# Parts of both halves stacked a batch ahead, expert rows loaded earlier, and a first layer whose sum is made by tokens

## The chip, the cores and the metric

The kernel runs on one NeuronCore of a Trainium2 chip, as one program. The metric is the device time in microseconds from start to end of one execution. A core has TensorE (matmuls and transposes into PSUM), VectorE, ScalarE, GpSimd and SyncE, which here only issues DMAs. The engines meet only at semaphores, and each runs its own instructions strictly in order.

## The reference, cut to what matters

```python
def layer0(x):                        # x: 8 x 512 x 128, layer-normed copy n; 16 heads of 8
    q, k, v = ...                     # q from n, k and v from a latent of 32; rope on q and k
    att = softmax(sum over d of q*k)  # for every token: 16 heads against 16 heads
    out = (att @ v) @ Wout + bout
    h = silu(n @ wg) * (n @ wu)       # hidden 384
    return x + out + h @ wd
def layer1(x1):
    u, z = split(norm(x1) @ in_proj)  # 256 channels each; u through a causal conv of 4 taps and silu
    dt = softplus(...)                # max(x,0) + ln(1 + exp(-|x|)), with a correction of rounding
    for t in tokens:                  # 256 channels x 16 states, a recurrence over 512 tokens
        h = exp(dt*A) * h + (dt*u) * B
        y = sum over states of h * C
    y = (y + u*D) * silu(z) @ out_proj
    return x1 + y + shared expert + the two best of 8 experts (sigmoid gates, sorted into tiles)
```

## The kernel before, in words

**Two layers, one after the other.** `layer0` walks the 8 batches of 512 tokens in a pipeline: iteration b makes the scores of batch b, the values, the gated hidden layer and the sum of batch b-1, and the next layer's norm, transposes and gate logits of batch b-2. All five engines have their lists of steps written out by hand. The sum of batch b-1 is made by channels (`project_out`: the attention and the three hidden blocks against `wout` and `wd`, 512 tokens wide, into the PSUM tile `p_acc`). ScalarE copies it and adds `bout` (`copy_sum`), TensorE transposes it back to tokens (`turn_back`, which stands behind `turn_x` and `latent` of batch b+2), and VectorE adds the residual (`add_up`, L704). VectorE also runs the routing of each group of four batches: `choose(0)` at the end of iteration 6, `place(0)` in iteration 7, `choose(1)` and `place(1)` at the end. GpSimd scatters the rows of group 0 to their experts' tiles in DRAM (`send(0, 0)` at the end of iteration 7, `send(0, 1)` at the end of iteration 8), 16 indirect DMAs each; `second_root` of the next iteration stands behind them in its queue.

**Layer 1** has a prologue for batch 1 and then, for every batch, 32 steps k. Step k works on one group of 128 (channel, state) rows by 512 tokens. TensorE spreads dt*u over the 16 states (`spread_du`, L1834, into one of two `p_du` buffers, one step ahead, free once `scan` k-1 is done). VectorE multiplies by B (`inject`, L1716) and runs the recurrence (`scan`, L1723). GpSimd multiplies by C (`times_c`, L1459), TensorE gathers. ScalarE exponentiates the decays two steps ahead (`decay`), from tiles of 1 MB that SyncE loads, 8 in a batch (`load_decays`), into 4 buffers.

dt*u is a float32 number that TensorE takes as three bfloat16 parts. `first_part` and `second_part` (ScalarE), `second_rest` (L1705) and `third_part` (L1710, VectorE) make them for one half of the channels at a time into `part`, and SyncE's `stack` moves them by 12 small DMAs into `block_in`. Half 0 of batch b+1 is made in steps 19 to 22 of batch b; half 1 in steps 5 to 8 of batch b+1 itself, since `part` and `block_in` have room for one of each.

The softplus of batch b+1 runs in steps 13 to 17: ScalarE's exponential, VectorE's 1 + e (`softplus_one`, L1691), ScalarE's logarithm, VectorE's `softplus_cut` and `softplus_end`.

**Expert tiles** run among the steps: each batch has two units of the shared expert and eight tiles of 256 routed rows, a unit every 3.2 steps. Each unit has a slot s, and its stages are placed around it: rows and weights are loaded at step s-11 (`load_tile`, SyncE: L1300 129 KB of rows, L1305 384 KB of weights), the rows are transposed at s-7 (L1850), gate at s-6, up at s-5, `half` (VectorE) at s-4, `hidden` (GpSimd) at s-3, `down` at s (L1883 for the shared expert), `weigh` (ScalarE) at s+1, and the result is stored at s+2. The last tile has slot 6 of batch 7. From step 9 of batch 7 GpSimd fetches the second group's results with 32 indirect DMAs (`fetch`, L1495); the first waits until all tiles are stored.

A wait at the head of an engine's list holds all that is behind it. TensorE's next `spread_du` stands behind the transposes and matmuls of the tiles, and SyncE's loads behind its waits for parts.

## Time and profile before

| | |
|---|---|
| time, median of 3 runs (lowest, highest) | 1319.91 us (1317.92, 1344.87) |
| the profiled execution's own time | 1330.25 us |
| its span in the trace | 1328.1 us |
| busy: TensorE, VectorE, ScalarE, GpSimd | 911.6, 943.1, 505.4, 709.4 us |
| mean granted clock of TensorE | 0.783 of full |
| layer 0 | 0 to 496 us |
| layer 1, prologue | 496 to 577 us |
| layer 1, batches: first scan of batch 1 to the last of batch 8 | 577.3 to 1308.9 us |
| DMA queue of SyncE | 183.0 MB |

The profiled execution is 10.3 us longer than the median of the runs; 2.15 us of its time lie outside the span. The first scans of the eight batches start at 577.3, 665.6, 764.0, 859.1, 957.9, 1049.0, 1145.2 and 1231.3 us, so a batch takes 79 to 99 us. Busy shares are averages: which wait ends last in a stretch has to be read there.

### The profile page before, as it was taken

What the parts mean: (1) busy time and instruction counts of PE and PEld (TensorE: products, weight loads), DVE (VectorE), ACT (ScalarE), POOL (GpSimd) and SP (SyncE); (2) the same over time, 40 slices, a digit from 0 to 9 for tenths busy, and PEclk for the clock granted to TensorE, in tenths of its full rate; (3) what the DMA queues carried; (4) which work ended last, traced back from release to release, by engine and by line L of the source; (5) the groups of instructions that cost most, each with busy time, mean ns of one, the idle gap of its engine ahead of it and who ended that gap; (6) DMA issues with size and microseconds to landing.
All of it is one profiled execution on the core that took longest, in us unless ns stands there. A gap on an engine that the chain in (4) does not pass through costs nothing. (4 is left out here: it accounts for less than half of the span.)

```text
span 1328.1 us, 12681 instructions
## 1 busy us (share of the span) xinstructions
PE 911.6 (69%) x3460; PEld 416.8 (31%) x3460; DVE 943.1 (71%) x1288; ACT 505.4 (38%) x842; POOL 709.4 (53%) x547
## 2 busy tenths in 40 slices
PE   4677877977768535447867876876886877754553
PEld 1222322322223211113534433543444534421110
DVE  3577786776867450157878788798689788789884
ACT  1112212312123111255556465474564565562320
POOL 1012102101064305635856666678688888779996
PEclk9668878779588666667987888997886887985655
DMA  4984664646431204366666666676785776655641
GB/s 138 217 173 112 149 177 130 154 137 149 106 108 35 70 24 148 85 160 194 158 159 174 156 174 171 179 182 162 162 212 162 165 180 175 193 137 129 140 123 28
DMA packets 102833, 192.23 MB, mean 145 GB/s; under 512 B 13259, under 2 KB 68108, under 8 KB 90348
## 3 DMA queue, kind: packets, MB, share of 16 engines
q1 hardware_dynamic: 91500, 183.00, 53.0%
q0 software_dynamic: 11264, 8.43, 3.6%
q8 instruction: 28, 0.46, 0.2%
q14 instruction: 41, 0.34, 0.1%
HBM read 146.74 MB, written 32.06 MB: 135 GB/s over the span
## 5 line engine op out<-in xcount | busy, mean ns | idle before, releaser
L1459 POOL TENSOR_TENSOR hc<-hs,c_rep 128x512 f32<-128x512 f32 x256 | 368.9, 1530 | 159.3 <-DVE hs L1723 158.7
L1716 DVE TENSOR_TENSOR p_du<-p_du,b_rep 128x512 f32<-128x512 f32 x256 | 175.4, 685 | 107.8 <-PE p_du L1834 107.7
L1834 PE MATMUL p_du<-block_in,spread 96*128 96x512 bf16 x256 | 116.6, 460 | 156.9 <-DVE hs L1723 126.5
L1723 DVE TENSOR_TENSOR_SCAN hs<-slots,p_du 128x512 f32<-128x512 f32 x128 | 156.3, 1221 | 14.3 <-POOL hc L1459 3.2
L1723 DVE TENSOR_TENSOR_SCAN hs<-decays,p_du 128x512 f32<-128x512 f32 x128 | 156.3, 1221 | 14.2 <-POOL hc L1459 2.7
L447 POOL TENSOR_TENSOR sc<-ex,ex_part 128x1024 f32<-128x1024 f32 x8 | 17.0, 2128 | 214.2 <-ACT ex_part L535 214.2
L679 DVE TENSOR_TENSOR value_prod<-p_eb,v 128x512 f32<-128x512 f32 x128 | 83.7, 684 | 46.4 <-PE p_eb L959 46.0
L1495 POOL DMA_INDIRECT y_xr<-moe_sums,position x64 | 104.9, 1640 | 16.3 <-issue 14.0
L1834 PEld LDWEIGHTS p_du<-block_in,spread 96*128 96x128 bf16 x256 | 26.1, 103 | 276.8 <-DVE hs L1723 200.2
L1591 ACT ACTIVATE decays<-decays,a_neg 128x512 f32<-128x512 f32 x128 | 87.5, 719 | 40.6 <-DMA decays<-dt_rows 40.6
L1843 PE MATMUL p_y<-hc,gather 128*32 128x512 f32 x512 | 84.8, 741 | 22.4 <-POOL hc L1459 22.4
L1471 POOL TENSOR_TENSOR y_hid<-y_hid,g_in 128x512 f32<-128x512 f32 x64 | 98.8, 1544 | 2.2 <-DVE y_hid L1736 2.2
L1806 PE MATMUL y_misc<-y_ht,wtap 128*128 128x512 f32 x128 | 75.4, 726 | 30.5 <-DVE a_neg L1685 14.7
L1591 ACT ACTIVATE slots<-slots,a_neg 128x512 f32<-128x512 f32 x128 | 88.7, 721 | 9.6 <-DMA slots<-dt_rows 9.5
L1603 ACT ACTIVATE g_in<-p_g 128x512 f32<-128x512 f32 x64 | 38.0, 594 | 121.7 <-PE p_g L1863 80.9
L655 DVE TENSOR_TENSOR score_prod<-qb,p_k 128x2048 f32<-128x2048 f32 x32 | 72.4, 2282 | 10.5 <-issue 5.3
L923 PE MATMUL p_s<-score_prod,sum_d 128*32 128x512 f32 x256 | 52.1, 900 | 28.6 <-DVE score_prod L655 25.4
L1863 PE MATMUL p_g<-xgt,wm 128*128 128x256 f32 x192 | 65.4, 473 | 5.5 <-DMA wm<-in_wmoe 3.7
L1597 ACT ACTIVATE xgt<-p_g 128x256 f32<-128x256 f32 x48 | 18.4, 384 | 132.6 <-PE p_g L1850 131.6
L457 POOL TENSOR_TENSOR root<-var,half 128x8 f32<-128x8 f32 x8 | 13.2, 1650 | 101.1 <-DVE var L727 101.0
L1890 PEld LDWEIGHTS p_o<-wm,y_hid 128*128 128x128 f32 x384 | 63.4, 236 | 10.9 <-issue 8.1
L1890 PE MATMUL p_o<-wm,y_hid 128*128 128x128 f32 x384 | 62.7, 317 | 0.0
(186 smaller groups left out, 1711.9 us busy)
## 6 DMA issues: line engine op xcount, KB each, us to landing
qb<-rq_rows SPq DMA_DIRECT2D x32, 1024.0 KB, 13.4
decays<-dt_rows SPq DMA_DIRECT2D x32, 1024.0 KB
slots<-dt_rows SPq DMA_DIRECT2D x32, 1024.0 KB
wm<-in_wmoe SPq DMA_DIRECT2D x48, 384.0 KB
moe_rows<-zeros SPq DMA_DIRECT2D x8, 774.0 KB, 6.4
xg<-moe_rows SPq DMA_DIRECT2D x48, 129.0 KB, 14.0
stack<-ex_part SPq DMA_DIRECT2D x96, 64.0 KB
block_in<-y_part SPq DMA_DIRECT2D x192, 32.0 KB
```

The lines of the kernel that those rows point to most:

```text
L655: nc.vector.tensor_tensor(score_prod[:, i % 2], qb[:, i], p_k[:].unsqueeze(1).to_broadcast([128, 4, T]), ALU.mult)\
L679: nc.vector.tensor_tensor(value_prod[:, n % NP], p_eb[:, n % 2], v[:, b % NV], ALU.mult).then_inc(weighed.sem, 1)
L1459: nc.gpsimd.tensor_tensor(hc[:, k % NA], hs[:, k % 4], c_rep[:, p], ALU.mult).then_inc(hc_done.sem, 1)
L1471: nc.gpsimd.tensor_tensor(hid[:, v % 2], hid[:, v % 2], g_in[:, v % 2], ALU.mult).then_inc(hid_done.sem, 1)
L1495: nc.gpsimd.indirect_dma_start(xr[:, b - 1, t], None, moe["sums"][grp], bass.IndirectOffsetOnAxis(ap=position[:, grp, kk, TT * i + t:TT * ...
L1591: nc.scalar.activation(decay_of, decay_of, ACT.Exp, scale=a_neg[:, g:g + 1]).then_inc(da_done.sem, 1)
L1716: nc.vector.tensor_tensor(p_du[:, k % 2], p_du[:, k % 2], b_rep[:, p], ALU.mult).then_inc(dbu_done.sem, 1)
L1723: nc.vector.tensor_tensor_scan(hs[:, k % 4], decays[(8 * (b - 1) + k // 4) % NQ][:, bass.ts(j, T)], p_du[:, k % 2], 0.0, ALU.mult, ALU.add ...
L1806: ins = nc.tensor.matmul(p_misc[:], wtap[:, k, bass.ts(n, 128)], ht[:, b % 2, k:k + T], start=(k == 0), stop=(k == CONV - 1))
L1834: nc.tensor.matmul(p_du[:, k % 2], spread[:, i], block_in[:, s, j], start=True, stop=True).then_inc(du_full.sem, 1)
L1843: ins = nc.tensor.matmul(p_y[32 * j:32 * j + 32], w["gather"][:, i], hc[:, k % NA], start=(i == 0), stop=(i == 3))
L1890: ins = nc.tensor.matmul(p_o[:, bass.ts(i, 128)], hid[:, v % 2, 256 * f + 128 * i:256 * f + 128 * i + 128], wm[:, j % NR, 2 * FF1 + 128 * ...
```

## The change

In layer 0 the sum is made with tokens on the partitions: `attn` and `hid` become the stationary operands and the 128 columns of `wout` and `wd` move, 32 matmul passes of 128 columns instead of 8 of 512 (TensorE makes two passes of a float32 matmul). `copy_sum` and `turn_back` go. `bout`, loaded once into all partitions, is added to x by GpSimd (`add_bias`, a 128x512 float32 addition, issued a batch ahead, right behind `second_root`), and `add_up` waits for `p_acc` and this. Routing of group 0 moves one iteration later (`choose(0)` to 7, `place(0)`, `ranks(0)` and `send(0, 0)` to 8, `send(0, 1)` to 9); the gates `eg` get room for both groups.

In layer 1 `part` holds both halves and `block_in` three blocks, so half 1 of batch b+1 is made in steps 23 to 26 of batch b and stacked in SyncE's steps 25 to 27; the prologue makes both halves of batch 1. ScalarE adds the one (`one_more`, in step 14, with the logarithm right behind it), and `softplus_cut` and `softplus_end` run in steps 15 and 16. ScalarE exponentiates decays three steps ahead instead of two, and `load_decays` stands one step later. Rows are loaded at s-14, weights at s-12 into five buffers (before four), and results are stored at s+4 from three buffers (before s+2 from two).

Only changed lines are shown.

```diff
+            def add_bias(b):
+                if b == 1:
+                    pool.wait_ge(loaded0, 16 * n_small)
+                pool.wait_ge(ln_done.sem, ln_done.at(b))
+                nc.gpsimd.tensor_tensor(x[:, (b - 1) % NX], x[:, (b - 1) % NX], bout[:].unsqueeze(1).to_broadcast([128, TT, D]), ALU.add)\
+                    .then_inc(biased.sem, 1)
...
+                if b == 1:
+                    add_bias(1)
+                if b < B:
+                    add_bias(b + 1)
...
-                if b == 7:
+                if b == B:
-                if b == 8:
+                if b == B + 1:
...
-            def copy_sum(b):
-                act.wait_ge(acc_full.sem, acc_full.at(b))
-                act.wait_ge(back_full.sem, back_full.at(b - 1))
-                nc.scalar.activation(summed[:], p_acc[:], ACT.Identity, bias=bout[:, 0:1]).then_inc(acc_copied.sem, 1)
...
-                if b > 4:
-                    act.wait_ge(route.sem, route.at(1, 1))
-                i = TT * ((b - 1) % 4)
+                i = TT * (b - 1)
...
-                dve.wait_ge(back_full.sem, back_full.at(b))
+                dve.wait_ge(acc_full.sem, acc_full.at(b))
+                dve.wait_ge(biased.sem, biased.at(b))
...
-                nc.vector.tensor_scalar(g[:, 1], eg[:], 1.0, None, ALU.add).then_inc(route.sem, 1)
+                nc.vector.tensor_scalar(g[:, 1], eg[:, GT * grp:GT * grp + GT], 1.0, None, ALU.add).then_inc(route.sem, 1)
...
-                if b == 7:
+                if b == B:
-                if b == 6:
+                if b == B - 1:
...
-                    if b == 6:
+                    if b == B - 1:
...
-                nc.tensor.matmul(p_acc[:], wout[:], attn[:], start=True, stop=False)
-                for f in range(FT0):
-                    ins = nc.tensor.matmul(p_acc[:], wd[:, f], hid[:, f], start=False, stop=(f == FT0 - 1))
+                for t in range(TT):
+                    nc.tensor.matmul(p_acc[:, bass.ts(t, D)], attn[:, bass.ts(t, 128)], wout[:], start=(t == 0), stop=False)
+                    for f in range(FT0):
+                        ins = nc.tensor.matmul(p_acc[:, bass.ts(t, D)], hid[:, f, bass.ts(t, 128)], wd[:, f],
+                                               start=False, stop=(t == TT - 1 and f == FT0 - 1))
-            def turn_back(b):
-                pe.wait_ge(acc_copied.sem, acc_copied.at(b))
-                for t in range(TT):
-                    ins = nc.tensor.transpose(p_acc[:, bass.ts(t, 128)], summed[:, bass.ts(t, 128)], ident[:])
-                ins.then_inc(back_full.sem, 1)
...
-                if b == 7:
+                if b == B:
...
-        NR = 4
+        NR = 5
+        NO = 3
+        NB = 3
+        AHEAD = 3
-        part = sb("y_part", [128, 3, T], BF16)
-        block_in = sb("block_in", [96, ST, 4, T], BF16)
+        part = sb("y_part", [128, ST, 3, T], BF16)
+        block_in = sb("block_in", [96, NB, 4, T], BF16)
-        os = sb("os", [128, 2, 2, D])
+        os = sb("os", [128, NO, 2, D])
...
-            def load_tile(j, v):
+            def load_rows(j):
-                r = j % NR
+            def load_weights(j):
+                grp, i = divmod(j, NTILE)
+                r = j % NR
-                sp.dma_start(moe["sums"][grp][256 * i:256 * i + 256].rearrange("(s p) d -> p s d", p=128), os[:, j % 2])\
-                    .then_inc(os_out[j % 2].sem, 16)
+                sp.dma_start(moe["sums"][grp][256 * i:256 * i + 256].rearrange("(s p) d -> p s d", p=128), os[:, j % NO])\
+                    .then_inc(os_out[j % NO].sem, 16)
-                    sp.wait_ge(du_full.sem, du_full.at(b - 1, SEG * (s + 1)))
+                    if s:
+                        sp.wait_ge(du_full.sem, du_full.at(b - 1, SEG))
+                    else:
+                        sp.wait_ge(du_full.sem, du_full.at(b - 2))
-                    sp.dma_start(block_in[32 * i:32 * i + 32, s, c], part[32 * c:32 * c + 32, i]).then_inc(stacked[s].sem, 16)
+                    sp.dma_start(block_in[32 * i:32 * i + 32, (2 * b + s) % NB, c], part[32 * c:32 * c + 32, s, i]).then_inc(stacked[s].sem, 16)
...
+                for i in range(3):
+                    stack(1, 1, i)
-                    for _, _, j, v in due(b, k, 11):
+                    for _, _, j, _ in due(b, k, 14):
-                            load_tile(j, v)
-                    if new and k % 4 == 1 and k < 20:
-                        load_decays(b, (k + 11) // 4)
-                    if nxt and k % 4 == 1 and k > 20:
-                        load_decays(b + 1, (k - 21) // 4)
-                    if new and k in (6, 8, 9):
-                        stack(b, 1, (6, 8, 9).index(k))
-                    for _, _, j, _ in due(b, k, -2):
+                            load_rows(j)
+                    for _, _, j, _ in due(b, k, 12):
+                        if j is not None:
+                            load_weights(j)
+                    if new and k % 4 == 2 and k < 20:
+                        load_decays(b, (k + 10) // 4)
+                    if nxt and k % 4 == 2 and k > 20:
+                        load_decays(b + 1, (k - 22) // 4)
+                    for _, _, j, _ in due(b, k, -4):
+                        if k in (25, 26, 27):
+                            stack(b + 1, 1, k - 25)
-            for i in range(2):
-                sp.wait_ge(os_out[i].sem, os_out[i].at(NTILE))
+            for i in range(NO):
+                sp.wait_ge(os_out[i].sem, os_out[i].at(2 * NTILE // NO))
...
+            def one_more(b):
+                act.wait_ge(sp_exp.sem, sp_exp.at(b))
+                act.wait_ge(part3.sem, part3.at(b - 1))
+                nc.scalar.activation(wz, ez, ACT.Copy, bias=1.0).then_inc(sp_one.sem, 1)
-                before = stacked[0].at(b) if s else stacked[1].at(b - 1)
-                act.wait_ge(stacked[1 - s].sem, before)
-                nc.scalar.activation(part[:, 0], dtu[:, 1, s], ACT.Copy).then_inc(part1.sem, 1)
+                act.wait_ge(stacked[s].sem, stacked[s].at(b - 1))
+                nc.scalar.activation(part[:, s, 0], dtu[:, 1, s], ACT.Copy).then_inc(part1.sem, 1)
-                nc.scalar.activation(part[:, 1], rest[:, s], ACT.Copy).then_inc(part2.sem, 1)
+                nc.scalar.activation(part[:, s, 1], rest[:, s], ACT.Copy).then_inc(part2.sem, 1)
...
-                act.wait_ge(os_out[j % 2].sem, os_out[j % 2].at(j // 2))
+                act.wait_ge(os_out[j % NO].sem, os_out[j % NO].at(j // NO))
-                    ins = nc.scalar.activation(os[:, j % 2, i], p_o[:, bass.ts(i, 128)], ACT.Copy, scale=xg[:, j % NX, i, D:D + 1])
+                    ins = nc.scalar.activation(os[:, j % NO, i], p_o[:, bass.ts(i, 128)], ACT.Copy, scale=xg[:, j % NX, i, D:D + 1])
+                one_more(1)
-                first_part(1, 0)
-                second_part(1, 0)
+                for s in range(ST):
+                    first_part(1, s)
+                for s in range(ST):
+                    second_part(1, s)
-                decay(1, 0)
-                decay(1, 1)
+                for k in range(AHEAD):
+                    decay(1, k)
-                    if new and k + 2 < GROUPS:
-                        decay(b, k + 2)
-                    if nxt and k + 2 >= GROUPS:
-                        decay(b + 1, k + 2 - GROUPS)
+                    if new and k + AHEAD < GROUPS:
+                        decay(b, k + AHEAD)
+                    if nxt and k + AHEAD >= GROUPS:
+                        decay(b + 1, k + AHEAD - GROUPS)
...
-                    if new and k == 5:
-                        first_part(b, 1)
-                    if new and k == 7:
-                        second_part(b, 1)
-                    if k == 15:
+                    if k == 14:
+                        one_more(b + 1)
-                    if k == 19:
-                        first_part(b + 1, 0)
-                    if k == 21:
-                        second_part(b + 1, 0)
+                    if k in (19, 23):
+                        first_part(b + 1, (k - 19) // 4)
+                    if k in (21, 25):
+                        second_part(b + 1, (k - 21) // 4)
-            start(dve, [sp_one, sp_step, rest1, part3, dbu_done, scanned, y1_done, half_done, res_done])
+            start(dve, [sp_step, rest1, part3, dbu_done, scanned, y1_done, half_done, res_done])
...
-            def softplus_one(b):
-                dve.wait_ge(sp_exp.sem, sp_exp.at(b))
-                dve.wait_ge(part3.sem, part3.at(b - 1))
-                nc.vector.tensor_scalar(wz, ez, 1.0, None, ALU.add).then_inc(sp_one.sem, 1)
...
-                    if new and k == 6:
-                        second_rest(b, 1)
-                    if new and k == 8:
-                        third_part(b, 1)
-                    if k == 14:
-                        softplus_one(b + 1)
-                    if k == 17:
+                    if k == 16:
-                    if k == 20:
-                        second_rest(b + 1, 0)
-                    if k == 22:
-                        third_part(b + 1, 0)
+                    if k in (20, 24):
+                        second_rest(b + 1, (k - 20) // 4)
+                    if k in (22, 26):
+                        third_part(b + 1, (k - 22) // 4)
...
-                nc.tensor.matmul(p_du[:, k % 2], spread[:, i], block_in[:, s, j], start=True, stop=True).then_inc(du_full.sem, 1)
+                nc.tensor.matmul(p_du[:, k % 2], spread[:, i], block_in[:, (2 * b + s) % NB, j], start=True, stop=True).then_inc(du_full.sem, 1)
```

## Rows read from the trace of the kernel before

**Rows 1.** Busy time by stretch: us, each engine (instructions), granted clock, DMA share, GB/s.
```profile
0.00:496.00 496.00, 353.06 (x1284) 127.97 (x1284) 327.58 (x628) 100.95 (x137) 97.66 (x81) 0.79 0.50 126
496.00:577.00 81.00, 35.88 (x50) 11.96 (x50) 7.96 (x11) 21.54 (x29) 37.91 (x38) 0.65 0.42 119
...
764.00:858.00 94.00, 71.83 (x308) 40.53 (x308) 74.71 (x83) 54.34 (x98) 61.23 (x49) 0.87 0.66 174
...
957.00:1048.00 91.00, 73.41 (x308) 42.14 (x308) 78.32 (x85) 54.22 (x98) 81.24 (x61) 0.83 0.70 181
1048.00:1144.00 96.00, 74.32 (x308) 42.85 (x308) 77.55 (x85) 54.11 (x98) 81.24 (x60) 0.82 0.71 176
...
1176.00:1328.00 152.00, 71.18 (x245) 22.13 (x244) 119.48 (x120) 42.48 (x66) 136.05 (x98) 0.60 0.47 108
```

**Rows 2.** VectorE's costliest groups in the second layer: count, busy, mean ns, idle before.
```profile
L1716 DVE TENSOR_TENSOR p_du<-p_du,b_rep 128x512 f32<-128x512 f32 x256 | 175.4, 685 | 107.8 <-PE p_du L1834 107.7
L1723 DVE TENSOR_TENSOR_SCAN hs<-decays,p_du 128x512 f32<-128x512 f32 x128 | 156.3, 1221 | 14.2 <-POOL hc L1459 2.7 <-issue 0.4
...
L1710 DVE TENSOR_TENSOR y_part<-conv,y_part 128x512 bf16<-128x512 f32 x15 | 26.5, 1769 | 1.1 <-ACT y_part L1582 1.0
L1705 DVE TENSOR_TENSOR conv<-dtu,y_part 128x512 f32<-128x512 f32 x15 | 24.6, 1637 | 0.0
...
L1691 DVE TENSOR_SCALAR conv<-dtu 128x1024 f32<-128x1024 f32 x7 | 12.3, 1752 | 4.0 <-ACT dtu L1568 4.0
```

**Rows 3.** VectorE by time: start, us, line, and in brackets the idle time before it.
```profile
610.28 0.70 DVE L1716 TENSOR_TENSOR p_du<-p_du,b_rep 128x512 f32<-128x512 f32 x1 [5.97 <-PE p_du L1834]
...
670.42 0.70 DVE L1716 TENSOR_TENSOR p_du<-p_du,b_rep 128x512 f32<-128x512 f32 x1 [3.58 <-PE p_du L1834]
...
1027.32 0.70 DVE L1716 TENSOR_TENSOR p_du<-p_du,b_rep 128x512 f32<-128x512 f32 x1 [2.19 <-PE p_du L1834]
...
1031.01 0.70 DVE L1716 TENSOR_TENSOR p_du<-p_du,b_rep 128x512 f32<-128x512 f32 x1 [1.68 <-PE p_du L1834]
...
1151.97 0.70 DVE L1716 TENSOR_TENSOR p_du<-p_du,b_rep 128x512 f32<-128x512 f32 x1 [2.15 <-PE p_du L1834]
...
1179.71 0.70 DVE L1716 TENSOR_TENSOR p_du<-p_du,b_rep 128x512 f32<-128x512 f32 x1 [2.57 <-PE p_du L1834]
```

**Rows 4.** TensorE by time, end of batch 1: waits for a tile's rows and weights.
```profile
669.26 0.69 PE L1850 MATMUL p_g<-ident,xg 128*128 128x128 f32 x2 [4.79 <-DMA xg<-moe_rows]
...
671.80 2.07 PE L1863 MATMUL p_g<-xgt,wm 128*128 128x256 f32 x4 [1.42 <-DMA wm<-in_wmoe]
```

**Rows 5.** SyncE's queue by time in the same stretch: its issues.
```profile
641.39 7.57 SPq L1322 DMA_DIRECT2D block_in<-y_part  x12
...
652.51 0.35 SPq L1300 DMA_DIRECT2D xg<-moe_rows  x1
...
654.29 0.36 SPq L1305 DMA_DIRECT2D wm<-in_wmoe  x1
```

**Rows 6.** First load of decays: SyncE issues it, ScalarE begins on it.
```profile
557.88 0.61 SPq L1351 DMA_DIRECT2D decays<-dt_rows  x1
...
572.36 2.56 ACT L1591 ACTIVATE decays<-decays,a_neg 128x512 f32<-128x512 f32 x4 [4.04 <-DMA decays<-dt_rows]
```

**Rows 7.** VectorE in the first layer: `add_up` as a group, and one wait by time.
```profile
L704 DVE TENSOR_TENSOR x<-p_acc,x 128x512 f32<-128x512 f32 x8 | 5.5, 692 | 29.3 <-PE p_acc L1003 27.7 <-issue 1.6
...
443.51 0.16 DVE L731 TENSOR_TENSOR rr<-root 128x4 f32<-128x4 f32 x1 [8.09 <-POOL root L457]
```

**Rows 8.** TensorE by time: the same work in 512-column and in 128-column matmuls.
```profile
215.37 2.74 PE L997 MATMUL p_acc<-hid,wd 128*128 128x512 f32 x6
...
803.98 1.05 PE L1883 MATMUL p_acc<-shared_w,y_hid 128*128 128x128 f32 x8
```

**Rows 9.** One line of the first layer: ns min/median/max of its instructions.
```profile
L739 DVE TENSOR_SCALAR xnr<-x,mv,rr x32: 332/341/1207, 130.1 to 481.5; 128x128 f32<-128x128 f32 x32
```

**Rows 10.** GpSimd by time: the first fetch of the second set of tokens.
```profile
1176.25 1.57 POOL L1495 DMA_INDIRECT y_xr<-moe_sums,position  x1 [5.98 <-issue]
```

50 lines of the change are left out of this document (24 added, 26 removed).

## Prediction

> **What bounds the kernel now.** First I read the busy time by stretch [rows 1]. The first layer takes 496 us with VectorE busy 328 and TensorE 353, so neither is full and waits set the time. In a middle batch VectorE is busy 75 of 94 us, TensorE 72. From batch 4 on GpSimd's fetches come in: it is busy 81 of 91 us in batch 5, 81 of 96 in batch 6, and 136 of the last 152 us. So the second layer is VectorE's until batch 3, VectorE's and GpSimd's together to step 9 of batch 7, and GpSimd's from there.
>
> Then VectorE's groups in the second layer [rows 2]. A step costs 0.69 + 1.22 us, 61 us a batch. The 107.8 us that it idled before `inject`, all for TensorE, are the largest thing to win. 20.1 of them lie ahead of the first scan; 87.7 are left. By time [rows 3] they fall into three kinds. At step 12 of a batch: seven waits from 5.97 us (610.28) to 2.57 (1179.71), 22.4 in all. Around the batch's turn (steps 30 to 2) and at step 24: sixteen from 3.58 (670.42) to 2.15 (1151.97), 43.9 in all. The rest, about 21, follow step 24, as the 1.68 at 1031.01, where TensorE has the next convolution's matmuls.
>
> Why the second kind? TensorE's rows by time [rows 4] show it waiting 4.79 us for a tile's rows and 1.42 more for its weights; `spread_du` stands behind. SyncE issued them at 652.51 and 654.29 [rows 5], 16.7 and 17.5 us before use. They are planned 4 and 5 steps (10 to 13 us) ahead of that use, and stand behind 7.57 us of small DMAs for `stack` [rows 5]. Step 24 of batch 5 waits 2.19 us (1027.32) without such a DMA wait, so that much of each of five belongs to matmuls.
>
> **The change part by part.**
>
> *Rows at s-14, weights at s-12.* Rows get 7 steps before their use, 17 to 18 us at 2.5 us a step, against the 16.7 measured; weights 6 steps, 15 us, against 17.5. So rows are in time, weights about 2 us late at the four or five batch turns. Of 43.9 us, 5 x 2.19 = 11 stay as matmuls and 8 turn into waits for weights: 25 us gained, between 8 (the supply is no faster) and 33. The later store and the fifth and third buffers cost nothing: they take waits from SyncE's list, and `down` of tile j-5 lies four steps before its reload. If the weights were still not free, SyncE would hold the decays behind them.
>
> *The one on ScalarE.* Seven instructions of VectorE go, 12.3 us, and 4.0 of waiting for the exponential [rows 2]. The new wait, `softplus_cut` for `one_more`, stands before VectorE's next `inject`. The exponential used to end about 0.5 us after VectorE was ready for it; now a decay (0.7) and the addition (about 1.1, as the exponential of this size) follow, while VectorE has step 15 (1.9) to run. So a wait of at most 0.5, and none where a `half` stands in between. ScalarE is busy 54 of 94 us and takes the 1.1. GpSimd's `steps` come earlier by what `softplus_end` gains. One instruction lies in GpSimd's stretch. Gain 15, between 8 and 17.
>
> *Half 1 a batch ahead.* L1710 and L1705 cost 1.77 and 1.64 us [rows 2]. In steps 6 and 8 of batches 1 to 7 VectorE has no idle time, so 7 x 3.4 = 24 us leave. They come back at steps 24 and 26, beside waits of 1.68, 0.95 and 0.89 us for TensorE's convolution, 3.5 a batch (the first of them stands in [rows 3]). I let 9 us come back, as not all fits and batch 7 has no convolution. Gain 15, between 0 (TensorE's lag is made up by cover that I take away at steps 6 and 8) and 24. If that cover were gone, 3.4 a batch would stand on the path. SyncE now waits in steps 25 to 27 for parts that ScalarE and VectorE make in steps 23 to 26, with rows, weights and decays queued behind. ScalarE's wait in step 25 for `second_rest` has decays behind it, which are three steps ahead. The wait of `spread_du` 16 for its block goes; what was late next there was VectorE itself. In the prologue part 2 of half 0 starts some 1.7 us later behind `first_part` of half 1, while SyncE is still issuing part 1: 0, at most 3.
>
> *Decays.* A load has 7 steps until ScalarE wants it, before 9. The first took 14.5 us from issue to use [rows 6], 7 steps are 17. So 0; the rival below says when not.
>
> *Step 12.* There TensorE runs gate, projection, `down` and gather between two `spread_du`. In rows at full clock this fits, in those at 1.2 GHz it doesn't: the clock in these stretches fell after TensorE had idled. Fewer waits may keep it up. Bounds 0 and 22; I take 6, nearer to nothing, as no row shows the clock kept.
>
> These make 25 + 15 + 15 + 6 = 61. But GpSimd's 81 busy us are a floor for batches 5 and 6 [rows 1], which would otherwise come to 80; near two full engines waits add. I take 6 off: **55**.
>
> *From step 9 of batch 7.* The first fetch waits for the last tile's store, 5.98 us [rows 10]. The store no longer stands behind two stacks but behind `scan` 7: 1.4 us earlier. Then GpSimd's 136 of 152 us stand, of which the change takes only waits for `steps`, about 1 us. Gain 2, between -4 (the store is placed later) and 6.
>
> *First layer.* `add_up` idled 29.3 us [rows 7]. In iterations 2 to 6 it was 4.4, 3.1, 4.9, 4.4 and 4.2, since `turn_back` stands behind `turn_x` and `latent`. The sum is ready before VectorE's `normalize` ends, so these go; TensorE itself starts the next scores only 1 to 3 us earlier. I take 3 each: 15. In iterations 7 to 9 copy and transposes (1.6 us with their hand-overs) go, the matmuls grow: eight wide passes of some 0.46 (2.74 for six) become 32 of 0.13 (1.05 for eight), 3.7 to 4.2 us [rows 8]. 0.9 each: 2.7; earlier the 0.5 is hidden, at half clock about 1.4 would be. The scatters used to hold `second_root` in two iterations, 3.4 and 8.09 us [rows 7]; one iteration later only iteration 9 is held, by 7: 4.4 gained, and `send(0, 1)` ends some 9 us before the last `second_root` needs GpSimd. The routing's instructions are the same. Against it: `add_bias`, 1.2 us each on GpSimd, 8 times, starts just when VectorE begins `slots` and `xnr`. In the one place where a GpSimd addition met these, an instruction of 341 ns took 1207 [rows 9]. Five such meetings of 0.87: 4 us, between 0 and 6. Sum 15 + 2.7 + 4.4 - 4 = **18**, between 6 and 28.
>
> By the Trainium skill (SBUF, State Buffer: Who interferes with whom) VectorE and GpSimd share a pair of ports that is locked for a whole instruction. The 1207 ns agree with it; five full blocks of 1.2 would make 6, not 4, so it speaks against this part, and the forecast would be 2 us longer.
>
> **Sum.** 55 + 2 + 18 = 75. The profiled execution took 1330.25 us, 10.3 above the median, so 1255 for such an execution and **1245** for the median 1319.9.
>
> **The rivals.**
> (1) *Supply takes the place.* Rows and weights come earlier but share the queue with the same megabytes in less time, and SyncE's 24 stack DMAs now stand in steps 21 to 27, just before the batch turn. For it: 7.57 us for 12 of them [rows 5], and 163 to 181 GB/s through all batches [rows 1], of which shorter batches need up to a tenth more. Then the first part gives 8 and step 12 nothing: 55 - 17 - 6 = 32, in all 52: 1268; with the moved parts also uncovered (nothing from them) 1283.
> By the Trainium skill (DMA: Bandwidth & Descriptors, Issuing engines are not separate dma queues) all issues run on the same 16 engines and interleave, so an earlier issue buys place, not rate. The trace's 16.7 us for 129 KB agrees.
> (2) *Nothing moves in the second layer*, as TensorE at half clock and GpSimd bound it: only 18 + 2 + 7 from the softplus: 1293, no change by measurement.
> (3) *Slower: decays late.* SyncE loads them a step later and ScalarE needs them a step earlier. From issue to use over 10 steps (25 us: 7 of lead and the 3 that ScalarE is ahead) every scan group of four waits. At 28 us the price is 3 us for each of some 48 loads, 144 us, less the 75: about 1389. Against it: 14.5 us [rows 6], and no wait of ScalarE for decays in batches 2 to 7.
> That stacking ahead doesn't happen, because SyncE reaches it late, ends as rival 1.
>
> **How the numbers follow.** Chances: forecast 0.66, rival 1 0.22, rival 2 0.08, rival 3 0.04. All steps at their good ends would give 1196 (96 less 6 for GpSimd, 6 and 28), but they share one floor, GpSimd's, so I set the low end at 1215. The high end takes in rival 1 with its second form and stops short of rival 2: 1287. About 2% is what a measurement of this kernel can tell from no change, so 1293.5 divides. Faster: the forecast and nearly all of rival 1, 0.86; the same, 0.09; slower 0.05.
>
> **What would show it.** Right: `add_up` idles under 1 us in iterations 2 to 6 and the second layer begins at 475 to 482 us; L1850 waits for rows under 10 us in all instead of 46; no `softplus_one` on VectorE and no wait above 0.5 for `one_more`; L1705 and L1710 in steps 24 and 26, with the waits there smaller; batches 2 to 6 at 82 to 87 us; from the first fetch to the end still about 150 us. Wrong: TensorE's waits move from L1850 to L1863 (weights) or ScalarE waits for decays (rivals 1, 3); waits at step 12 grow once VectorE is faster; `xnr` and `slots` stretch in every iteration.

## The result, and the profile after

| | before | after |
|---|---|---|
| time, median of 4 runs (lowest, highest) | 1318.91 us (1316.89, 1344.87) | 1260.13 us (1251.83, 1268.29) |
| the profiled execution's own time | 1330.25 us | 1268.29 us |
| its span, granted clock | 1328.1 us, 0.783 | 1266.5 us, 0.813 |
| first scan of batch 1 | 577.3 us | 544.0 us |
| first scan of batch 1 to the last of batch 8 | 731.6 us | 703.3 us |

The ratio is 0.9559, with a 95% interval of 0.9463 to 0.9655: faster by 59 us, where 75 were forecast. The forecast was 1245 us in a range of 1215 to 1287. Its two halves are both off. By the two profiled executions, which are 62 us apart, the part up to the first scan gained 33 us instead of 18, the rest 28 instead of 57.

Busy time by stretch, in the columns of [rows 1] (TensorE, its weight load, VectorE, ScalarE, GpSimd, clock, DMA share, GB/s): first layer, prologue, batches 3 to 6 and the end from the second set of fetches:

```profile
0.00:460.00 460.00, 324.39 (x1434) 132.33 (x1435) 327.17 (x615) 95.41 (x129) 107.39 (x89) 0.83 0.54 136
460.00:544.00 84.00, 34.85 (x64) 11.82 (x61) 11.48 (x25) 23.74 (x32) 37.66 (x38) 0.66 0.39 112
...
720.00:805.00 85.00, 67.67 (x309) 39.19 (x308) 72.58 (x84) 55.33 (x99) 63.15 (x49) 0.90 0.68 190
805.00:903.00 98.00, 67.84 (x313) 38.65 (x312) 82.49 (x83) 55.36 (x100) 74.20 (x56) 0.90 0.66 169
903.00:995.00 92.00, 69.87 (x307) 40.19 (x306) 80.15 (x85) 55.52 (x99) 82.98 (x63) 0.89 0.72 184
995.00:1082.00 87.00, 67.75 (x311) 39.49 (x310) 78.89 (x84) 55.42 (x100) 81.66 (x62) 0.90 0.72 190
...
1110.00:1266.00 156.00, 68.48 (x226) 20.87 (x226) 111.97 (x117) 40.94 (x62) 136.53 (x98) 0.58 0.45 102
```

Batches 2 and 3 take 85 us and the sixth 87, as forecast (82 to 87), but the fourth takes 98 and the fifth 92. The clock is 0.90 where it was 0.82 to 0.87. The last stretch has the same work on GpSimd and isn't longer: its window here begins 5.4 us before the first fetch of the second set, that of [rows 1] with it. From this fetch to the end it is 151.1 us, before 151.8.

The groups that answer to [rows 2, 7]: in the second layer VectorE's `inject` (L1726) and `scan` (L1733), and TensorE's transposes of rows (L1855) and gate matmuls (L1868); in the first layer `add_up` (L708) and VectorE's first instruction after `second_root` (L735). Columns: count, busy, mean ns, idle before and what ended it.

```profile
L1726 DVE TENSOR_TENSOR p_du<-p_du,b_rep 128x512 f32<-128x512 f32 x256 | 175.2, 684 | 62.4 <-PE p_du L1839 62.0
L1733 DVE TENSOR_TENSOR_SCAN hs<-slots,p_du 128x512 f32<-128x512 f32 x128 | 156.2, 1220 | 40.6 <-POOL hc L1471 27.0 <-ACT slots L1607 2.5 <-issue 0.9
...
L1855 PE MATMUL p_g<-ident,xg 128*128 128x128 f32 x96 | 20.2, 294 | 0.0
...
L1868 PE MATMUL p_g<-xgt,wm 128*128 128x256 f32 x192 | 61.3, 448 | 47.1 <-ACT xgt L1613 28.6 <-DMA wm<-in_wmoe 18.3
...
L708 DVE TENSOR_TENSOR x<-p_acc,x 128x512 f32<-128x512 f32 x8 | 5.5, 686 | 4.6 <-PE p_acc L1002 4.6
...
L735 DVE TENSOR_TENSOR rr<-root 128x4 f32<-128x4 f32 x8 | 4.7, 589 | 10.7 <-POOL root L464 10.7
```

Of these, the groups of rows, of weights and of the instruction after `second_root` in the kernel before:

```profile
L1850 PE MATMUL p_g<-ident,xg 128*128 128x128 f32 x96 | 23.7, 335 | 46.2 <-DMA xg<-moe_rows 46.1
L1863 PE MATMUL p_g<-xgt,wm 128*128 128x256 f32 x192 | 65.4, 473 | 5.5 <-DMA wm<-in_wmoe 3.7 <-ACT xgt L1597 1.2
...
L731 DVE TENSOR_TENSOR rr<-root 128x4 f32<-128x4 f32 x8 | 1.3, 158 | 13.2 <-POOL root L457 9.8 <-issue 3.4
```

`inject` idles 62.4 us instead of 107.8, and the waits for rows (46.1 in all before) are gone. Waits for weights went from 3.7 to 18.3. Three things are new. TensorE waits 28.6 us for `xgt`, ScalarE's copy of a tile's transposed rows, where it waited 1.2. VectorE's `rr` takes 589 ns in the mean instead of 158. Both come up again below. And `scan` waits 27.0 us for buffers that GpSimd frees, before 3.2 in the same group. Where this comes from stands in GpSimd's and SyncE's rows by time (start, us, and for an engine its idle time before):

```profile
844.96 1.64 POOL L1507 DMA_INDIRECT y_xr<-moe_sums,position  x1 [16.69 <-issue]
...
1115.35 1.57 POOL L1507 DMA_INDIRECT y_xr<-moe_sums,position  x1 [12.74 <-DMA moe_sums<-os]
```

```profile
1097.85 0.79 SPq L1358 DMA_DIRECT2D decays<-dt_rows  x1
1098.75 2.18 SPq L1315 DMA_DIRECT2D moe_sums<-os  x1
1101.12 0.59 SPq L1358 DMA_DIRECT2D decays<-dt_rows  x1
1102.55 0.37 SPq L1315 DMA_DIRECT2D moe_sums<-os  x1
```

The first fetch of each set stands 16.7 and 12.7 us for the last tile's store, before 0.8 and 5.98 [rows 10]. VectorE's two largest stalls of this kind, 11.8 us in batch 4 and 7.7 in batch 7, lie right behind. And SyncE's own list, which I had not looked at in the kernel before. Its waits in the second layer, before:

```profile
SPq L155 <- ACT os L1610: 96.9, 26, 11.1
...
SPq L155 <- ACT y_part L1582: 29.5, 8, 7.9
...
SPq L155 <- ACT y_part L1578: 9.3, 5, 4.0
```

and after (us in all, times, longest):

```profile
SPq L155 <- ACT os L1626: 19.2, 11, 2.6
```

136 us of waiting for tiles' results and for parts were 19 after the change. Much of what follows turns on these rows, but not on their sum: by the experiments the 39 us for parts matter, and most of the 78 us less for results don't.

### The profile page after: what moved, and what is told of

Same layout as the page of the kernel before. It is cut to its first block and busy times, and to the rows that moved or that the text cites. A ratio compares the mean times of both kernels' runs of the same rounds, so it can differ in the third digit from the quotient of the medians.

```text
span 1266.5 us, 13006 instructions
## 1 busy us (share of the span) xinstructions
PE 856.6 (68%) x3620; PEld 407.2 (32%) x3620; DVE 934.0 (74%) x1280; ACT 509.3 (40%) x842; POOL 722.6 (57%) x555
## 5 line engine op out<-in xcount | busy, mean ns | idle before, releaser
L1471 POOL TENSOR_TENSOR hc<-hs,c_rep 128x512 f32<-128x512 f32 x256 | 377.4, 1591 | 114.1 <-DVE hs L1733 113.7
L1726 DVE TENSOR_TENSOR p_du<-p_du,b_rep 128x512 f32<-128x512 f32 x256 | 175.2, 684 | 62.4 <-PE p_du L1839 62.0
L1839 PE MATMUL p_du<-block_in,spread 96*128 96x512 bf16 x256 | 111.4, 441 | 126.8 <-DVE hs L1733 119.5
L1733 DVE TENSOR_TENSOR_SCAN hs<-slots,p_du 128x512 f32<-128x512 f32 x128 | 156.2, 1220 | 40.6 <-POOL hc L1471 27.0
L1733 DVE TENSOR_TENSOR_SCAN hs<-decays,p_du 128x512 f32<-128x512 f32 x128 | 156.2, 1220 | 14.0 <-POOL hc L1471 3.0
L1507 POOL DMA_INDIRECT y_xr<-moe_sums,position x64 | 108.5, 1696 | 39.2 <-issue 25.1
L1868 PE MATMUL p_g<-xgt,wm 128*128 128x256 f32 x192 | 61.3, 448 | 47.1 <-ACT xgt L1613 28.6
L1895 PEld LDWEIGHTS p_o<-wm,y_hid 128*128 128x128 f32 x384 | 59.5, 225 | 12.7 <-issue 10.8
L1895 PE MATMUL p_o<-wm,y_hid 128*128 128x128 f32 x384 | 59.6, 307 | 0.9 <-ACT os L1626 0.9
L1868 PEld LDWEIGHTS p_g<-xgt,wm 128*128 128x128 f32 x192 | 39.5, 220 | 60.7 <-issue 35.1
L927 PE MATMUL p_s<-score_prod,sum_d 128*32 128x512 f32 x256 | 46.3, 805 | 17.4 <-DVE score_prod L658 17.4
## 6 DMA issues: line engine op xcount, KB each, us to landing
wm<-in_wmoe SPq DMA_DIRECT2D x48, 384.0 KB, 13.8
xg<-moe_rows SPq DMA_DIRECT2D x48, 129.0 KB, 13.7
```

Of the source, the lines that this page charges most:

```text
L1471: nc.gpsimd.tensor_tensor(hc[:, k % NA], hs[:, k % 4], c_rep[:, p], ALU.mult).then_inc(hc_done.sem, 1)
L1507: nc.gpsimd.indirect_dma_start(xr[:, b - 1, t], None, moe["sums"][grp], bass.IndirectOffsetOnAxis(ap=position[:, grp, kk, TT * i + t:TT * ...
L1726: nc.vector.tensor_tensor(p_du[:, k % 2], p_du[:, k % 2], b_rep[:, p], ALU.mult).then_inc(dbu_done.sem, 1)
L1733: nc.vector.tensor_tensor_scan(hs[:, k % 4], decays[(8 * (b - 1) + k // 4) % NQ][:, bass.ts(j, T)], p_du[:, k % 2], 0.0, ALU.mult, ALU.add ...
L1839: nc.tensor.matmul(p_du[:, k % 2], spread[:, i], block_in[:, (2 * b + s) % NB, j], start=True, stop=True).then_inc(du_full.sem, 1)
L1868: ins = nc.tensor.matmul(p_g[:, bass.ts(f, 256)], wm[:, j % NR, bass.ts(f, 128)], xgt[:, j % 2], start=True, stop=True)
```

## The experiments

All twelve ran in three sets of four, each set beside runs of the kernel before; sets 1 and 2 on one chip, set 3 on another. One thing has to be known to read the times. In all eight profiles of the first and third set VectorE stood still 13.6 to 13.8 us in iteration 8 of the first layer, and VectorE and ScalarE 4.6 to 6.9 us each in iteration 9; in the second set, and in the profile above, not once. The changed kernel took 1255.4 us in the second set and 1282.4 in the third, and of the 31 us between their profiled executions 21 lie ahead of the first scan (541.9 and 563.1). So a time is compared inside its set, and beside it I give the second layer's length from the profile (first scan to last), which the stall doesn't touch: 731.6 us before, and 703.3, 691.0 and 701.0 in three profiles of the changed kernel, 698 on average. The profiled execution is a single one and can lie far from the median: 11 us above it in the kernel before, 8 above in the changed kernel's first profile, 12 above with all stores at s+2 and with leads of 11, 16 and 17 below with the stores first in the step and the last store early. A difference of under 10 us in the last column says nothing, and with such an execution one of 20 says little. Set 1 has no run of the changed kernel itself.

| kernel | set | time, us | ratio to before (95%) | profiled execution | second layer |
|---|---|---|---|---|---|
| first layer alone | 1 | 1309.7 | 0.993 (0.988 to 0.998) | 1308.5 | 728.8 |
| all stores at s+2 | 1 | 1280.8 | 0.971 (0.966 to 0.976) | 1293.1 | 709.1 |
| stores first in the step | 1 | 1279.6 | 0.971 (0.962 to 0.979) | 1263.3 | 686.2 |
| leads of 11 | 1 | 1312.1 | 0.987 (0.979 to 0.995) | 1324.0 | 742.8 |
| changed kernel | 2 | 1255.4 | 0.952 (0.938 to 0.965) | 1254.1 | 691.0 |
| 64 increments more | 2 | 1279.7 | 0.972 (0.955 to 0.988) | 1272.6 | 700.6 |
| routing at its old place | 2 | 1264.6 | 0.965 (0.953 to 0.978) | 1262.6 | 690.4 |
| leads alone | 2 | 1299.3 | 0.984 (0.969 to 1.000) | 1296.1 | 726.6 |
| changed kernel | 3 | 1282.4 | 0.963 (0.956 to 0.969) | 1285.1 | 701.0 |
| half 1 in its own batch | 3 | 1319.6 | 0.997 (0.992 to 1.002) | 1316.3 | 736.6 |
| the one on VectorE | 3 | 1285.9 | 0.965 (0.956 to 0.975) | 1284.0 | 701.4 |
| last store early | 3 | 1273.0 | 0.951 (0.943 to 0.958) | 1256.3 | 675.0 |

**First layer alone.** The changed `layer0` with `layer1` as before.

> The new first layer with the old second layer. From the two traces the first layer now ends 33 us earlier (463.5 against 496.3 us), where 18 were forecast. If that is the first layer's own gain, this kernel takes 1319 - 33 = 1286 us (1280 to 1292). If the forecast's 18 were right and 15 of the 33 came from the profiled execution's higher clock alone (0.83 against 0.79 in this stretch), it takes about 1301. Either way its second layer looks like the old one: about 46 us of waits for a tile's rows, batches of 88 to 99 us.

Measured 0.993, some 10 us: neither 1286 nor 1301. The profile's first scan is at 558.6 (before 577.3), with the stall in it. The second layer is the old one, with 39.8 us of waits for rows. Without the stall the same first layer had the first scan at 544.0, 541.9 and 548.3 in three profiles: 29 to 35 us gained. With it all eight have it at 555.8 to 563.1: 14 to 22. Whether the higher clock of the stretch made part of the 33 isn't shown.

The forecast's price for `add_bias` is in these layers too, at an instruction for which it wasn't forecast: not `xnr` or `slots`, but the small product `rr` ahead of them. The two by time, in the changed kernel:

```profile
169.84 1.27 POOL L459 TENSOR_TENSOR x<-x,bout 128x512 f32<-128x512 f32 x1
170.28 0.85 DVE L735 TENSOR_TENSOR rr<-root 128x4 f32<-128x4 f32 x1
```

In iterations 2 to 6 `rr` takes 0.84 to 0.85 us instead of 0.16. It begins 0.44 us behind the addition and ends within 0.03 us of it, each time: 3.5 us in all, where 4 were forecast.

**The leads.** One experiment takes the longer lead away, one leaves it alone with the new first layer.

```diff
# leads of 11, in the changed kernel
-                    for _, _, j, _ in due(b, k, 14):
+                    for _, _, j, _ in due(b, k, 11):
                             load_rows(j)
-                    for _, _, j, _ in due(b, k, 12):
+                    for _, _, j, _ in due(b, k, 11):
                             load_weights(j)
```

> The changed kernel with rows and weights loaded at step s-11 as before (five buffers kept). The forecast gave the longer lead 25 us (8 to 33). If the 46 us of waits for rows were the path, they come back in part and this takes 1268 to 1293, about 1280. If the waits for the stacked parts (12 small DMAs that stood between rows and use) had been the cause, moving those alone was enough and this is within 5 us of the changed kernel.

> The new first layer, and the old second layer with one part of the change alone: rows loaded at s-14, weights at s-12 into five buffers. The kernel with everything but the longer lead took 1312 us, the one with none of the second layer's changes 1310: so my theory is that the lead is nearly the whole gain, about 45 us where I had forecast 25, and the two parts taken from VectorE give little: 1268 to 1280. Rival: the parts only pay together (the moved stacks free the queue that the earlier rows need): then the lead alone gives 15 to 25, 1285 to 1295.

Leads alone is the old second layer with `NR = 5` and rows and weights at 14 and 12. Without the lead the time is 1312.1 against 1280 for its neighbours of the set, and TensorE waits 68.1 us for rows, more than before the change. But the lead alone gives nothing either: 726.6 against 728.8. My theory for it fell. The rival's mechanism held, that the parts only pay together, and its 15 to 25 us for the lead alone did not. TensorE's groups, without the lead and with it alone:

```profile
L1855 PE MATMUL p_g<-ident,xg 128*128 128x128 f32 x96 | 22.8, 325 | 68.1 <-DMA xg<-moe_rows 68.1
```

```profile
L1867 PE MATMUL p_g<-xgt,wm 128*128 128x256 f32 x192 | 66.1, 477 | 36.7 <-DMA wm<-in_wmoe 35.5 <-ACT xgt L1601 0.8
```

The rows' waits have become waits for weights. (In its batches TensorE also waits 27.4 us for the stacked parts, 12.0 in the kernel with the first layer alone.) SyncE's queue in the kernel with leads alone, steps 22 to 29 of batch 2, shows why:

```profile
698.05 0.66 SPq L1297 DMA_DIRECT2D xg<-moe_rows  x1
705.35 0.64 SPq L1352 DMA_DIRECT2D decays<-dt_rows  x1
706.45 0.36 SPq L1312 DMA_DIRECT2D moe_sums<-os  x1
707.02 5.04 SPq L1323 DMA_DIRECT2D block_in<-y_part  x8
713.31 0.37 SPq L1306 DMA_DIRECT2D wm<-in_wmoe  x1
```

Between 698.7 and 713.3 us no tile's data is issued: SyncE waits 6.6 us ahead of its decays, then issues the parts. The weights that leave at 713.3 are used at 721.4, after 4.6 us of TensorE's waiting. A longer lead in the plan is no lead if the list is held ahead of the load.

**Half 1 in its own batch.** The parts of half 1 back in steps 5 to 8, their stacks in SyncE's steps 6, 8 and 9; prologue accordingly; all else as changed.

```diff
-                        if k in (25, 26, 27):
-                            stack(b + 1, 1, k - 25)
+                    if new and k in (6, 8, 9):
+                        stack(b, 1, (6, 8, 9).index(k))
```

> The changed kernel, but half 1 of the parts is made and stacked in its own batch again (steps 5 to 8, SyncE's steps 6, 8 and 9). The lead alone gave 2 to 5 us in the second layer and the parts without the lead less than nothing, together about 40. Theory: what pays is SyncE's list. With half 1 back, its 12 small DMAs and the waits for its parts stand in steps 6 to 9 again, before rows and weights that are needed there; VectorE gets 3.4 us a batch back at steps 6 and 8. The forecast's value of the moved half was 15 us; by my theory now 15 to 25: 1272 to 1282. Rival: the later store (SyncE's waits for the tiles' results fell from 97 to 19 us) is what frees the list, and half 1 is worth nothing: 1255 to 1262.

Measured 1319.6 against 1282.4: 37 us, the whole gain of the second layer (736.6) and more than my theory's 15 to 25. SyncE's waits:

```profile
SPq L155 <- ACT os L1624: 44.1, 10, 8.5
...
SPq L155 <- ACT y_part L1592: 27.0, 7, 6.4
SPq L155 <- ACT y_part L1596: 19.9, 8, 5.1
```

47 us of waits for parts stand in the list again (none in the changed kernel), and those for results are up from about 19 to 44. ScalarE's waits for decays are 92.5 us against 76.1 beside it, GpSimd's for the stores 19.0 and 18.2 against 12.7 and 14.6. Of the 36 us by which the second layer is longer VectorE idles 22 and is busy 13 more. 10 of the 13 are in its instructions for the parts themselves (L1715 and L1720, 26.6 and 28.6 us instead of 20.2 and 24.6, the same 32 instructions). So the place on VectorE, on which I had put the value, is about a third of it; that the list makes the rest is read from these waits, and no run parts the two.

**The one on VectorE.** `softplus_one` in step 14 and `softplus_end` in 17 again, ScalarE's logarithm in step 15.

> The changed kernel with the softplus's one added by VectorE again (steps 14, 15 and 17). Forecast: 15 us (8 to 17) from 12.3 us of VectorE's work and 4 of waiting, so 1270. Rival: in steps 13 to 17 the time is set by TensorE and the tiles, or VectorE's gain is taken up by a wait behind it: 1255 to 1262.

Measured 1285.9 against 1282.4, and 701.4 against 701.0: nothing, as the rival had it. The 12 us are on VectorE again, and its idle time in the second layer is shorter instead (100 against 115 us). Its `inject` in this kernel and in the changed kernel of the set:

```profile
L1724 DVE TENSOR_TENSOR p_du<-p_du,b_rep 128x512 f32<-128x512 f32 x256 | 175.1, 684 | 53.6 <-PE p_du L1840 53.0 <-issue 0.4
```

```profile
L1726 DVE TENSOR_TENSOR p_du<-p_du,b_rep 128x512 f32<-128x512 f32 x256 | 175.3, 685 | 71.8 <-PE p_du L1839 71.5
```

The list of ScalarE shows where the gain goes. From step 14 of batch 2 of the changed kernel (third set), ScalarE, and the gate matmul that waits for `xgt`:

```profile
683.52 1.04 ACT L1585 ACTIVATE conv<-dtu 128x1024 f32<-128x1024 f32 x1
684.58 1.28 ACT L1589 ACT_TABLE_LOAD   x1
685.87 1.06 ACT L1589 ACTIVATE conv<-conv 128x1024 f32<-128x1024 f32 x1
686.95 1.28 ACT L1607 ACT_TABLE_LOAD   x1
688.24 0.72 ACT L1607 ACTIVATE decays<-decays,a_neg 128x512 f32<-128x512 f32 x1
688.87 0.36 ACT L1613 ACTIVATE xgt<-p_g 128x256 f32<-128x256 f32 x1
...
689.38 2.05 PE L1868 MATMUL p_g<-xgt,wm 128*128 128x256 f32 x4 [4.50 <-ACT xgt L1613]
```

and with the one on VectorE:

```profile
684.91 0.36 ACT L1608 ACTIVATE xgt<-p_g 128x256 f32<-128x256 f32 x1
685.29 1.28 ACT L1584 ACT_TABLE_LOAD   x1
...
687.58 1.91 PE L1869 MATMUL p_g<-xgt,wm 128*128 128x256 f32 x4
```

`one_more` (L1585) and the logarithm right behind it (L1589), with a table load on either side, stand 4.7 us ahead of a 0.36 us copy, and TensorE and its next `spread_du` wait for that copy. It comes back in five or six of the batches of every kernel with the one on ScalarE: TensorE waits 19.5 to 35.8 us for `xgt` there, and VectorE 4.6 to 9.7 us at its `inject` of step 18. In the four kernels with the one on VectorE these are 2.3 us at most and 0. The addition and the earlier logarithm moved together, so which of the two does it isn't parted.

**The stores.** Three forms: all at s+2 as before; all at s+4 but first in SyncE's step; and only the last tile of each group at s+2 and first in the step.

```diff
# last store early
+                    for _, _, j, _ in due(b, k, -2):
+                        if j is not None and j % NTILE == NTILE - 1:
+                            store_tile(j)
                     for _, _, j, _ in due(b, k, 14):
...
-                        if j is not None:
+                        if j is not None and j % NTILE != NTILE - 1:
                             store_tile(j)
```

> The changed kernel, but a tile's results are stored at step s+2 again (three buffers kept). Theory: GpSimd's first fetch of each group waits for the last tile's store (16.7 and 12.7 us in the changed kernel), because at s+4 the store is issued right behind a 1 MB load of decays in the same step of SyncE; at s+2 the wait falls to 1 to 6 us as before. The rest of batch 7 and 8 is GpSimd's, so the second wait counts nearly in full and the first in part: 8 to 16 us faster than the changed kernel, about 1248. Rival: the fetches just wait earlier and GpSimd's work is not on the path: within 3 us of the changed kernel.

> The changed kernel with the store still at step s+4, but issued as the first thing of that step of SyncE, ahead of the step's load of decays, rows and weights. It parts two causes of GpSimd's wait at the first fetch: if the queueing behind the megabyte of decays makes it (theory), the wait falls to 4 to 6 us and the time to 1246 to 1252; if it is the two steps of lateness (5 us), the wait falls only from 12.7 to about 11 and the time stays within 3 us of the changed kernel.

> The changed kernel with one difference: the last tile of each group is stored at step s+2 as the first thing in SyncE's step; all others stay at s+4. Storing all at s+2 gave 1281 and left GpSimd's wait before the first fetch at 13.1 and 12.3 us, since SyncE then waits for results ahead of its loads. Theory: GpSimd's wait before the first fetch of each group falls from 11 to 14 us to 4 to 8, SyncE's list stays free, and as GpSimd sets the time from there, 6 to 12 us are gained: 1244 to 1250. Rival: the stores' landing is limited by the megabytes in flight, the wait stays and the time too (1255).

All at s+2: 1280.8 us, with GpSimd still waiting 13.1 and 12.3 us, so the theory fell; the longer wait at the first fetch isn't the later store's. First in the step: 1279.6, and the waits are 11.9 and 6.2. The two times are alike, and like the 1282.4 of the changed kernel in set 3 with the same stall: neither a gain nor a loss is shown, and the layers of 709.1 and 686.2 belong to executions 12 us above and 16 below their medians. This also weighs SyncE's waits. Those for results are 79.6 us with all stores at s+2 and 55.7 with the stores first in the step, against 19.2 in the changed kernel. Most of what the later store took out of the list is back, and the time isn't longer. The row of the first of the two:

```profile
SPq L155 <- ACT os L1626: 79.6, 28, 5.5
```

Last store early: 1273.0 against 1282.4, with intervals of the ratio that overlap by a little (0.956 to 0.969, 0.943 to 0.958), so a gain isn't shown clearly. Its six runs lie in two groups, 1256 to 1264 and 1282 to 1298, and the profiled one, with the second layer of 675.0, is the lowest. Its waits are still 12.2 and 9.8 us, not 4 to 8, so my theory explains 5 of the 26 us at most by which this layer is shorter than its neighbour's:

```profile
1103.11 1.57 POOL L1510 DMA_INDIRECT y_xr<-moe_sums,position  x1 [9.82 <-DMA moe_sums<-os]
```

SyncE had issued this store by 1092.7 us, ahead of the load of decays at 1092.9. That it stands behind a megabyte of its own step is therefore not the whole reason that it lands late, though the wait did fall to 6.2 us with the stores first in the step. The page of the changed kernel gives 14.6 us as the median from issue to landing of all 48 stores of 128 KB. In the kernel before, the last store was issued 9.6 us after the last issue of decays and 5.0 us ahead of the fetch that waits for it [rows 10]; in the changed kernel two megabytes were issued in the 5 us ahead of it.

```profile
1171.23 0.52 SPq L1311 DMA_DIRECT2D moe_sums<-os  x1
```

So what is in flight already looks like the cause; no run here takes it away. The rest of the 26 us is `inject`'s wait (43.9 instead of 71.8; 61.2 and 62.4 in the other profiles of the changed kernel) and stays unexplained.

**Routing at its old place.** `choose(0)` in iteration 6, `place(0)`, `ranks(0)` and `send(0, 0)` in 7, `send(0, 1)` in 8, with the new sum.

> The changed kernel with the routing of the first group at its old place (chosen at the end of iteration 6, sent at the end of 7 and 8), but the new sum by tokens and the gates with room for both groups. The forecast gave the move of the routing 4.4 us and the sum by tokens 14. If that is right, this loses 4 us against the changed kernel without the stall; scatters then lie in iterations 7 and 8, where second_root waits 3 and 8 us. If the stall of 13.7 us comes with scatters in iteration 8, it goes away here, and this is up to 10 us faster than the changed kernel with it.

1264.6 against 1255.4, with intervals that overlap. In the profiles the last `add_up` comes at 450.4 us, before the change at 473.9, so the sum by tokens gives 23.5 us. With the later routing and no stall it comes at 441.3 and 441.6 in the changed kernel and at 445.9 in the kernel with leads alone, whose first layer is the same: 4.5 to 9 us for the routing, each from one profile. No stall came in this set, so whether the old place would have kept clear of it isn't shown.

**The stall.** The changed kernel ran twice more, and once with idle instructions put in.

```diff
             statistics(2)
+            for _ in range(64):
+                hold(dve)
```

> The changed kernel once more, beside the experiments on one chip. In four profiles with its first layer (the kernels with one part undone) VectorE stood still for 13.6 to 13.8 us before the sum of batch 7, in iteration 8, although the sum had been ready since some 9 us and nothing else of what it waits for was open; in the profile of the changed kernel it did not. If this stall belongs to that first layer in general, this run shows it too, and the time is 1268 to 1280 instead of 1260. If the first profile was the rule, 1255 to 1265 and no stall.

> The changed kernel with 64 idle semaphore increments more in VectorE's stream, in its wait of 8 us for the second batch of x at the start. Theory: the stall of 13.7 us before the sum of batch 7 is VectorE waiting for its next block of instructions, which the DMA engines bring while GpSimd's 16 scatters run; the block's border then lies elsewhere in the stream (64 instructions earlier, before the scatters start), so no stall there: 10 to 14 us shorter than the unshifted kernel, if no other border falls among scatters. Rival: the stall belongs to the instruction itself (a port shared with GpSimd, a wait for the scatters): it stays where it is, 13.7 us, and the time is that of the unshifted kernel or 2 us more.

> The changed kernel a third time, as the yardstick of the three kernels beside it on the same chip. From its two earlier sets (1260 and 1255 us): 1250 to 1265. VectorE's stall of 13.7 us in iteration 8 was in all four profiles of one call and in none since, so I expect none.

The first repeat (second set) had no stall, as one of its two cases said. The second (third set) had it, against my expectation, and took 1282.4 us instead of 1250 to 1265. VectorE by time in the changed kernel, third set and second set:

```profile
399.19 3.36 DVE L701 RECIPROCAL rden<-p_a 128x512 f32<-128x512 f32 x1 [0.26 <-DVE attn L694]
416.12 0.69 DVE L708 TENSOR_TENSOR x<-p_acc,x 128x512 f32<-128x512 f32 x1 [13.58 <-remote]
```

```profile
399.65 0.69 DVE L708 TENSOR_TENSOR x<-p_acc,x 128x512 f32<-128x512 f32 x1 [0.32 <-PE p_acc L1002]
```

The same instruction with the same inputs. In the third set its last matmul ended at 402.8 us; VectorE began 13.3 us later, 2.95 us after GpSimd was done with its 16th scatter (413.17). In all eight profiles with the stall this distance is 2.9 to 3.2 us:

```profile
412.20 0.97 POOL L483 DMA_INDIRECT moe_rows<-slots,position  x1 [0.31 <-issue]
```

So no packet is recorded that VectorE could have waited for. The kernel with 64 instructions more was to tell, and ran in the set without a stall: undecided. Its median is 24 us above its neighbour's, with intervals that overlap; in the profiles it is 18.5 us, 9 of them up to the first scan and 10 in batch 1, which I can't explain either.

## Why the prediction was right, and where it was not

The time was in the range and the sign right, but the sum of 75 holds by errors that cancel.

- **Leads: 25 (8 to 33).** Taking them away costs 31 us in time (1312.1 against 1280.8 and 1279.6 in its set). The waits for rows fell from 46.1 to nothing, where I left "8 turn into waits for weights" (15 did). The step that failed is the one before: I priced the lead by itself, in steps of 2.5 us, from the plan. By itself it is worth 2 us in the profiles, which is nothing by this measure.
- **Half 1: 15 (0 to 24).** Worth 37 with the lead in place, outside its bounds. The step "so 7 x 3.4 = 24 us leave" counts VectorE, whose busy time is 13 of the 36 us in the profiles; for the rest the rows show 12 small DMAs a batch and 47 us of SyncE's waiting for parts that no longer stand ahead of rows, weights and decays.
- **The one on ScalarE: 15 (8 to 17).** Worth 0 to 4. The step that failed is "ScalarE is busy 54 of 94 us and takes the 1.1": it looks at ScalarE's share and not at what stands behind in its list. 4.7 us of softplus now hold the copy `xgt` and with it TensorE (27.4 us of waits, 2.3 with the one on VectorE), and VectorE waits 18 us more before `inject` in the neighbouring profiles, 8.0 of them at step 18 alone. Two profiles of the changed kernel differ by 11 there, so the 18 is rough.
- So the terms didn't add: the second layer without the lead and that without the moved half are as long as before, with both it is about 33 us shorter, since both pass the same list. The sum 25 + 15 + 15 + 6 less 6 has 55 where 28 to 41 were measured.
- **Step 12: 6 (0 to 22).** 22.4 before; in the profile above 9.1 in batch 1 and at most 1.4 in each of the others, 13.7 in all. The clock rose, 0.90 instead of 0.82 to 0.87, and 9 us went. That the one made the other isn't shown: with all stores at s+2 the same waits are 24.9 us.
- **The later store: 0, and "1.4 us earlier" for the first fetch.** The 0 held: the later store takes some 78 us of waiting from SyncE's list, and with 60 of them back the time isn't longer. The 1.4 us was wrong: the first fetch waits 6.8 us longer in batch 7 and 15.9 in batch 4, and not because of the later store, as it waits about as long without it. From the first fetch on nothing changed (151.1 against 151.8 us), so the term "gain 2, between -4 and 6" was about -6.
- **First layer: 18 (6 to 28).** 29 to 35 without the stall, 14 to 22 with it. The sum by tokens, 17.7 less 4, gave 23.5: in the four iterations without routing 5.25 us each and not 3, at a clock of 0.83 instead of 0.79. The five meetings of `add_bias` came and cost 3.5 us of the 4, at `rr` and not at `xnr` or `slots`; `xnr` has its two instructions of 1.2 us after the change as before, both beside GpSimd's `xr`. The routing's 4.4 were 4.5 to 9. The wait for `second_root` was 8.94 us (forecast 7) and `add_up` idles 0.32 us in iteration 8.
- **Decays: 0.** Held: ScalarE's waits for them rose from 50.0 to 73.6 us, most of it in batches 1 and 8, with ScalarE three steps ahead of use; `scan` waits 2.5 us for them.
- **The rivals.** (1), supply takes the place, is what the kernel with the lead alone shows, where the waits for rows become waits for weights; in the full change it is only the 15 us more of waits for weights. (2) and (3) didn't happen. None of the rivals has ScalarE's list in it.

## What to carry to other kernels

Before a load is placed earlier, read what the issuing queue itself waits for: a load's real lead starts when the queue gets past the waits ahead of it, and parts that free the same queue are worth nothing one by one and a lot together, so their gains can't be added. The sum of a queue's waits is no measure: 60 us of waiting for results came back at no cost, 47 us of waiting for parts, ahead of weights and decays, came back with 37 us of time. Work moved to an engine that is half idle costs what stands behind it in that engine's list: read the list around the new place, step by step, for short instructions that others wait for. And compare a kernel with its own variants inside one set of runs, and with the place of the profiled execution among its runs: the same kernel took 1255 and 1282 us here, on two chips.

## What the runs showed of the hardware

- An engine can stand still for 13.6 us for something that isn't in its program's waits, in every profile of some sets of runs and in none of others, while GpSimd issues 16 scatters, and goes on 2.9 to 3.2 us after the last. Cause open.
- The 128 KB stores took 14.6 us at the median to land in the changed kernel, whose DMA moved 169 to 190 GB/s in batches 3 to 6; before, one with little in flight ahead of it had landed after at most 5.0 us.
- A VectorE instruction that meets a 128x512 addition of GpSimd can stand until this is done: `rr`, 128x4, took 0.84 to 0.85 us instead of 0.16 in all five meetings, ending with the addition, and `xnr`, 128x128, 1.2 us instead of 0.34 in two.
- ScalarE loaded a table of 1.28 us before the logarithm and again before the exponential behind it.
